# Attention in a four-layer kernel: score banks regrouped into two rings of three, exponentials taken in halves

## The chip, the cores and the metric

One core of one Trainium2 chip runs the whole program. The metric is the device time of one execution in microseconds. The kernel before took 611.96 us in the median of three runs (610.57 to 614.04).

## The reference, cut to what matters

Four layers follow each other on x of shape 16 x 128 x 256; each adds its result, scaled by tanh of a gate, to x: a WKV recurrence, a ternary feed-forward layer, a cross attention, a mixture of eight experts. The change is in the third:

```python
# target: layernorm(x), source: ctx; per batch 128 channels x 256 positions; HEADS = 16, HEAD_DIM = 8
q = einsum('oc,bct->bot', Wq, target) + bq     # k and v the same way from source
dot = einsum('bhdt,bhds->bhts', q, k) / sqrt(HEAD_DIM)
mask = target_mask[:, :, :, None] * source_mask[:, :, None, :]
dot = mask * dot - (1.0 - mask) * NEG
amap = softmax(dot, axis=-1) * mask
out = einsum('bhts,bhds->bhdt', amap, v)
```

So a batch has 16 heads, each with a 256 x 256 matrix of scores.

## The kernel before, in words

**Phases.** Up to about 180 us the first two layers run. The attention runs from there to about 447 us, its first two batches' scores beside the end of the feed-forward layer (the prologue). The experts follow.

**Attention by batch.** Every score is computed twice. First as rows by target position, in order that VectorE may take the maximum over the sources (`dve_reduce`, L907, one instruction for a head: 128 x 512 columns in, two maxima out). The negated maxima of a batch go through TensorE (`pe_mxT`, L841), ScalarE (`act_nm`, L975), GpSimd (`pool_np`) and memory and come back as three more rows of the stacked operand `QKA`. Then the scores are computed again, turned (rows by source position, the maximum already subtracted, `score_T`, L787), ScalarE takes the exponential (`act_exp`, L982) into `PT`, and TensorE multiplies by the values (`pe_pv`, L853), whose sums and products land in one bank, `PVB`.

**Order.** It is written by hand, as a slot for each batch b and pair p = 0 to 7; every engine walks the same slots in order (`turns`). The groups of batches 0 to 3 and 12 to 15 are unrolled, those between are a loop. In slot p of batch b TensorE does `pe_both`: the scores of heads n = 2p and 2p+1 (in the order of `head_of`) of batch b+2, and, between them matmul by matmul, four turned scores of batch b. Then it does `pe_pv` of two slots before, and in some slots one more piece of work, which shares the bank `MISC`: in slot 0 the maxima's transpose and before slot 1's pair the last value group of batch b-1, in slot 1 the projections of batch b+4 (L759, L763, the latter waits for VectorE's normalised row `Z3`, L893), in slot 3 the transpose of the result of b-1 (`pe_yT`, L862, after ScalarE's `act_qk`, L958, has read `MISC`), in slot 5 its transpose back (`pe_yo`, L869), in slot 6 the value projection (`pe_v`, L767, after VectorE's addition to X, L943). VectorE does two maxima in each slot and in slot 0 the statistics, in slot 1 `Z3`, in slot 3 and 4 the division (L918, L920, L926, L934, L938), in slot 5 the addition, in slot 7 `VF` (L899). ScalarE does one exponential in each slot, and `act_nm` in slot 0, `act_av` (L987) ahead of slot 1's, `act_qk` after slot 2's, `act_part` (L969) after slot 3's and 5's. The first `act_part` waits for GpSimd's masking of QK (L994), which waits for `act_qk`.

**Banks.** PSUM has eight banks of 512 fp32 columns. Before the change the scores for the maxima have two (`SBK`, banks 0 and 1, head n in bank n % 2). The turned scores have two double banks (`TBK`, banks 2 to 5, one double bank for a slot's four matrices). Banks 6 and 7 are `PVB` and `MISC`. `score_bank` lets TensorE write the scores of head n only when the maximum of head n-2 is taken (semaphore `a_red`); `turned_bank` lets it write a slot's turned scores when the exponential of two slots before is done (`a_exp`). In the last two batches there are no scores for maxima (`pe_scoresT`), and the layer norm of the experts and its transposes (L177) are in the slots.

Of the kernel before, what the change touches and what calls it, by code (L numbers as in the profile page):

```python
# [9 lines left out]
ACT = mybir.ActivationFunctionType  # L10
AX = mybir.AxisListType

P = 128
B, C = 16, 256
NG, GB = 4, 4
# [3 lines left out]
HEADS, HD = 16, 8  # L19
T = 256  # L20
# [29 lines left out]
def flamingo_kernel(nc, x, ctx, mask, g_xattn, g_ffn, time_decay, time_first, gate_wT, up_wT, down_wT,  # L50
# [10 lines left out]
    with ExitStack() as keep:  # L61
# [123 lines left out]
        with ExitStack() as part:  # L185
# [493 lines left out]
            with ExitStack() as att:  # L679
# [72 lines left out]
                def later(count):  # L752

                    return not isinstance(count, int) or count > 0
# [21 lines left out]
                def head_of(n):  # L776

                    return n // 2 + HALF * (n % 2)

                def score(pe, k, n, tt, SBK):  # L780
                    rows, h = rows_of(head_of(n))
                    return pe.matmul(SBK[n % 2][:, tt * T:(tt + 1) * T], QKA[rows, k, 0, h, tt * P:(tt + 1) * P],  # L782
                                     QKA[rows, k, 1, h, :], start=True, stop=True)

                def score_T(pe, k, i, st, j):
                    rows, h = rows_of(4 * j + i)
                    return pe.matmul(TBK[st][:, j * T:(j + 1) * T], QKA[rows, k, 1, h, st * P:(st + 1) * P],  # L787
                                     QKA[rows, k, 0, h, :], start=True, stop=True)

                def score_bank(pe, g, k, n):  # L790

                    b = GB * g + k
                    if n == 0:
                        pe.wait_ge(a_qa[k], 32 * (g + 1))
                    if later(HEADS * b + n - 1):
                        pe.wait_ge(a_red, HEADS * b + n - 1)

                def turned_bank(pe, g, k, i, st):

                    n = 8 * (GB * g + k) + 2 * i + st  # L800
                    if i == 0 and st == 0:
# [4 lines left out]
                def pe_scores(pe, g, k, p, SBK=SBK):  # L806

                    score_bank(pe, g, k, 2 * p)
                    score_bank(pe, g, k, 2 * p + 1)
                    for tt in range(2):  # L810
                        for n in (2 * p, 2 * p + 1):
                            last = score(pe, k, n, tt, SBK)
                            if tt == 1:
                                last.then_inc(a_s, 1)

                def pe_scoresT(pe, g, k, i, st):

                    turned_bank(pe, g, k, i, st)
                    for j in (0, 2, 1, 3):
                        last = score_T(pe, k, i, st, j)  # L820
                    last.then_inc(a_st, 1)

                def pe_both(pe, to_score, to_turn, p):


                    i, st = p // 2, p % 2
                    score_bank(pe, *to_score, 2 * p)
                    score(pe, to_score[1], 2 * p, 0, SBK)
                    turned_bank(pe, *to_turn, i, st)
                    score_T(pe, to_turn[1], i, st, 2)  # L830
                    score(pe, to_score[1], 2 * p, 1, SBK).then_inc(a_s, 1)
                    score_T(pe, to_turn[1], i, st, 3)
                    score_bank(pe, *to_score, 2 * p + 1)
                    score(pe, to_score[1], 2 * p + 1, 0, SBK)
                    score_T(pe, to_turn[1], i, st, 0)
                    score(pe, to_score[1], 2 * p + 1, 1, SBK).then_inc(a_s, 1)
                    score_T(pe, to_turn[1], i, st, 1).then_inc(a_st, 1)

# [5 lines left out]
                def pe_pv(pe, g, k, i, st):  # L844
# [5 lines left out]
                    grp = 0 if i < 3 else 1  # L850
                    pe.wait_ge(a_exp, 8 * b + 2 * i + st + 1)
                    for j in range(4):
# [48 lines left out]

                def dve_reduce(dve, g, k, n, SBK=SBK):
# [4 lines left out]
                    dve.tensor_reduce(MX[:, par, head_of(n), :], SBK[n % 2][:, :].rearrange("p (a s) -> p a s", a=2),  # L907
                                      axis=AX.X, op=ALU.max).then_inc(a_red, 1)
# [68 lines left out]
                def act_exp(act, g, k, i, st):  # L977
                    n = 8 * (GB * g + k) + 2 * i + st
# [913 lines left out]
```

## Time and profile before

| | |
|---|---|
| median of three runs | 611.96 us |
| the profiled execution | 612.62 us, of which the traced span is 610.9 us |
| TensorE / VectorE / ScalarE / GpSimd busy in the span | 83% / 67% / 37% / 34% |
| maxima (L907), 256 of 128 x 512 | 166.7 us, 682 ns each |
| exponentials (L982), 128 of 128 x 1024 | 129.9 us, 1023 ns each |
| scores (L782) and turned scores (L787), 512 matmuls each | 86.3 us and 84.9 us of TensorE's busy time |
| TensorE's clock over the span | 0.97 of full |

How to read it: the span is the trace's own clock from the first to the last instruction. Busy shares are over the whole program, four layers with different limits; what the change is worth has to be read inside the attention. An instruction's length in the trace can overlap its neighbour's on the same engine, so what an engine can do in a row is read from starts, not from lengths.

### The profile page before, as it was taken

How to read it: one execution, taken by the hardware profiler on the slowest of the kernel's cores; microseconds unless marked ns; L12 is line 12 of the kernel's file. 1: busy time of each engine (PE TensorE's matmuls, PEld its weight loads, DVE VectorE, ACT ScalarE, POOL GpSimd, SP SyncE). 2: the span in 40 equal slices, each digit the busy share in tenths (PEclk: the TensorE clock that was granted, in tenths of full speed). 3: DMA queues.
4: the chain of work that ended last, by engine and by line, in shares of the span. 5: the costliest groups of instructions: out<-in, count | busy, mean ns of one | idle time of the engine just before them, and what ended most of it. 6: DMA issues, size and time to landing. Idle time of an engine off the chain costs nothing. (4 is left out here: it accounts for less than half of the span.)

```text
span 610.9 us, 10613 instructions
## 1 busy us (share of the span) xinstructions
PE 508.4 (83%) x3368; PEld 269.3 (44%) x3368; DVE 407.8 (67%) x881; ACT 228.1 (37%) x330; POOL 205.7 (34%) x350
## 2 busy tenths in 40 slices
PE   1159899999798879999999998989879999899960
PEld 1034554644453433333333433333333555788850
DVE  4978678687535778888888888886946333333224
ACT  1003012031032027777777777767611010132310
POOL 2514115132265134554545545531210710022220
PEclk9999999999999969999999999999979999999995
DMA  6602006673228334555555555530040220266518
GB/s 165 213 1 69 1 0 134 88 188 141 58 70 224 87 93 134 154 148 148 149 138 140 137 136 153 140 83 7 3 141 2 103 69 0 66 187 190 185 40 275
DMA packets 70882, 68.11 MB, mean 111 GB/s; under 512 B 9136, under 2 KB 63328, under 8 KB 70848
## 3 DMA queue, kind: packets, MB, share of 16 engines
q1 hardware_dynamic: 69312, 63.48, 38.9%
q0 software_dynamic: 1536, 4.20, 1.9%
q8 instruction: 18, 0.29, 0.2%
q14 instruction: 16, 0.13, 0.1%
HBM read 41.04 MB, written 26.62 MB: 111 GB/s over the span
## 5 line engine op out<-in xcount | busy, mean ns | idle before, releaser
L907 DVE TENSOR_REDUCE MX<-psum 128x2 f32<-128x512 f32 x256 | 166.7, 682 | 32.0 <-PE psum L782 32.0
L982 ACT ACTIVATE HP<-psum 128x1024 f32<-128x1024 f32 x128 | 129.9, 1023 | 56.5 <-PE psum L787 54.6
L782 PE MATMUL psum<-QKA 60*128 60x256 bf16 x512 | 86.3, 279 | 21.0 <-DVE MX L907 19.4
L395 PE MATMUL psum<-space_a,space_w 128*128 128x512 f32 (+1 forms) x192 | 89.8, 616 | 5.0 <-ACT space_a L384 2.9
L787 PE MATMUL psum<-QKA 60*128 60x256 bf16 x512 | 84.9, 276 | 0.2 <-ACT HP L982 0.2
L853 PE MATMUL psum<-HP,VP 128*32 128x256 f32 x1024 | 81.8, 393 | 0.3 <-issue 0.2
L782 PEld LDWEIGHTS psum<-QKA 60*128 60x128 bf16 x512 | 33.5, 95 | 82.0 <-DVE MX L907 68.1
L395 PEld LDWEIGHTS psum<-space_a,space_w 128*128 128x128 f32 (+1 forms) x192 | 34.4, 187 | 49.1 <-issue 39.1
L431 PE MATMUL psum<-space_w,HP 128*128 128x256 f32 x192 | 50.8, 402 | 2.2 <-DVE HP L417 2.2
L1629 PE MATMUL psum<-space_a,wsh 128*128 (+3 forms) x96 | 45.2, 622 | 1.1 <-PEq L1120 1.1
L1703 PE MATMUL psum<-XT,WE 128*128 128x256 f32 (+1 forms) x192 | 44.1, 380 | 1.6 <-ACT XT L1584 1.6
L1557 POOL DMA_INDIRECT combined<-OE,to_u x16 | 15.3, 959 | 87.4 <-ACT OE L1597 85.0
L431 PEld LDWEIGHTS psum<-space_w,HP 128*128 128x128 f32 x192 | 33.9, 193 | 16.5 <-issue 12.4
L1703 PEld LDWEIGHTS psum<-XT,WE 128*128 128x128 f32 (+1 forms) x192 | 34.2, 181 | 8.2 <-issue 1.1
L403 ACT ACTIVATE space_a<-psum,hgs 128x512 f32<-128x512 f32 (+1 forms) x24 | 16.5, 686 | 56.5 <-PE psum L395 56.5
L1012 POOL TENSOR_TENSOR VP<-VF,maskT 128x32 f32<-128x32 f32 x128 | 25.9, 239 | 28.0 <-DVE VF L899 14.8
L145 POOL TENSOR_TENSOR rstd<-veps,neghalf 128x1 f32<-128x1 f32 (+1 forms) x21 | 15.7, 748 | 54.5 <-DVE veps L127 44.4
L787 PEld LDWEIGHTS psum<-QKA 60*128 60x128 bf16 x512 | 31.1, 95 | 6.1 <-issue 2.9
L994 POOL TENSOR_TENSOR QK<-QK,MB 128x512 f32<-128x512 f32 x16 | 20.3, 1268 | 40.0 <-ACT QK L958 40.0
L409 DVE SCALAR_TENSOR_TENSOR space_a<-space_a,psum 128x512 f32<-128x512 f32 (+1 forms) x24 | 16.1, 672 | 24.1 <-ACT space_a L403 24.1
L853 PEld LDWEIGHTS psum<-HP,VP 128*32 128x32 f32 x1024 | 20.4, 108 | 26.5 <-issue 22.0
L1837 DVE SCALAR_TENSOR_TENSOR H1s<-THs,psum 128x256 f32<-128x256 f32 (+1 forms) x24 | 10.1, 420 | 28.8 <-ACT THs L1591 27.8
(167 smaller groups left out, 710.3 us busy)
## 6 DMA issues: line engine op xcount, KB each, us to landing
QKA<-stack_scr SPq DMA_DIRECT2D x32, 480.0 KB, 5.3
stack_scr<-PARTS SPq DMA_DIRECT2D x32, 192.0 KB, 2.1
WE<-in_W SPq DMA_DIRECT2D x16, 352.0 KB
stack_scr<-PARTS SPq DMA_DIRECT2D x32, 128.0 KB, 1.9
dispatched<-zeros SPq DMA_DIRECT2D x8, 257.0 KB, 3.6
XD<-dispatched SPq DMA_DIRECT2D x8, 257.0 KB, 3.0
X<-in_x SPq DMA_DIRECT2D x4, 512.0 KB, 3.6
CV<-in_ctx SPq DMA_DIRECT2D x4, 512.0 KB, 4.6
```

The source lines that it names most:

```text
L395: last = pe.matmul(bank[2 * (i % 2) + side][0:m, :], (gw, uw)[side][:, h, i * P:i * P + m], ZT[:, h, :], start=(h == 0), stop=(h == 1))
L403: act.activation(TH[0:m, i % 2, :], bank[2 * (i % 2)][0:m, :], ACT.Tanh, scale=hgs[0:m, i:i + 1]).then_inc(s_th, 1)
L431: last = pe.matmul(DB[t // 2][:, (t % 2) * C:(t % 2 + 1) * C], HP[0:m, i, t * P:(t + 1) * P], dw[0:m, i, :], start=(i == 0), stop=(i == NI ...
L782: return pe.matmul(SBK[n % 2][:, tt * T:(tt + 1) * T], QKA[rows, k, 0, h, tt * P:(tt + 1) * P], QKA[rows, k, 1, h, :], start=True, stop=True)
L787: return pe.matmul(TBK[st][:, j * T:(j + 1) * T], QKA[rows, k, 1, h, st * P:(st + 1) * P], QKA[rows, k, 0, h, :], start=True, stop=True)
L853: last = pe.matmul(PVB[32 * j:32 * j + 32, grp * T:(grp + 1) * T], VP[:, k, st, 4 * j + i, :], PT[:, i % 2, st, j, :], start=(i in (0, 3) ...
L907: dve.tensor_reduce(MX[:, par, head_of(n), :], SBK[n % 2][:, :].rearrange("p (a s) -> p a s", a=2), axis=AX.X, op=ALU.max).then_inc(a_red, 1)
L982: act.activation(PT[:, i % 2, st, :, :].rearrange("p j t -> p (j t)"), TBK[st], ACT.Exp)\
L994: pool.tensor_tensor(QK2, QK2, MB[:, k, :].unsqueeze(1).broadcast_to([P, 2, T]), ALU.mult).then_inc(a_masked, 1)
L1012: last = pool.tensor_tensor(dst, src, maskT[:, st, bass.ds(b, 1)].unsqueeze(2) .broadcast_to([P, 4, 8]), ALU.mult)
L1629: last = pe.matmul(bank[2 * i + side][0:m, :], (wsh1, wsh3)[side][:, h, i * P:i * P + m], ZT4[:, h, bass.ds(GT * g, GT)], start=(h == 0), ...
L1703: last = pe.matmul(bank[i][0:m, lo:lo + CAP], w[:, s, h, i * P:i * P + m], XT[:, s, h, :], start=(h == 0), stop=(h == 1))
```

## The change: what it does

The scores for the maxima get three single banks (0, 1, 2), and the turned scores get three single banks (3, 4, 5), each bank holding two matrices. Both use the same order of banks in a batch, `THIRDS`: 0, 1, 2 over and over for the first fifteen, and bank 1 for the sixteenth. `last_use(n)` is the last earlier use of the same bank, counted over batches. It is three back nearly everywhere, two back for n = 15 and for n = 1 (which comes after the sixteenth of the batch before), and four back for n = 0 and n = 2. A slot's four turned matrices now lie in two banks, `half` = 1 first and `half` = 0 second, numbered by `turned_at`: 2p and 2p+1 in slot p. Each half has its own semaphore count in both directions: TensorE signals `a_st` after each half, ScalarE takes one exponential over 512 columns for each half (256 of them where there were 128), and TensorE waits for the half's bank alone. The order of the matmuls in `pe_both` is as before. In `pe_scoresT` both banks are waited for ahead of the four matmuls. The prologue keeps its two banks (`PRO`).

```diff
-                TBK = [psum[:, 2 * 512:4 * 512], psum[:, 4 * 512:6 * 512]]
+                THIRDS = [n % 3 for n in range(HEADS - 1)] + [1]
+                SBK3, TBK3 = bank[0:3], bank[3:6]
+                def last_use(n):
+                    return max(m for m in range(-HEADS, n) if THIRDS[m % HEADS] == THIRDS[n])
...
+                def turned_at(i, st, half):
+                    return 2 * (2 * i + st) + 1 - half
...
                 def score_bank(pe, g, k, n):
...
-                    if later(HEADS * b + n - 1):
-                        pe.wait_ge(a_red, HEADS * b + n - 1)
+                    score_filled(pe, g, k, n)
+                    pe.wait_ge(a_red, HEADS * (GB * g + k) + last_use(n) + 1)
...
-                def turned_bank(pe, g, k, i, st):
+                def turned_bank(pe, g, k, i, st, half):
...
-                    if later(n - 1):
-                        pe.wait_ge(a_exp, n - 1)
+                    if later(HEADS * b + last_use(m) + 1):
+                        pe.wait_ge(a_exp, HEADS * b + last_use(m) + 1)
...
                 def pe_scoresT(pe, g, k, i, st):
-                    turned_bank(pe, g, k, i, st)
-                    for j in (0, 2, 1, 3):
-                        last = score_T(pe, k, i, st, j)
-                    last.then_inc(a_st, 1)
+                    turned_bank(pe, g, k, i, st, 1)
+                    turned_bank(pe, g, k, i, st, 0)
+                    score_T(pe, k, i, st, 2)
+                    score_T(pe, k, i, st, 0)
+                    score_T(pe, k, i, st, 3).then_inc(a_st, 1)
+                    score_T(pe, k, i, st, 1).then_inc(a_st, 1)
...
                 def pe_both(pe, to_score, to_turn, p):
...
+                    for n, half in ((2 * p, 1), (2 * p + 1, 0)):
+                        to = SBK3[THIRDS[n]]
+                        score_bank(pe, *to_score, n)
+                        score(pe, to_score[1], n, 0, to)
+                        turned_bank(pe, *to_turn, i, st, half)
+                        score_T(pe, to_turn[1], i, st, 2 * half)
+                        score(pe, to_score[1], n, 1, to).then_inc(a_s, 1)
+                        score_T(pe, to_turn[1], i, st, 2 * half + 1).then_inc(a_st, 1)
...
                 def act_exp(act, g, k, i, st):
...
-                    act.wait_ge(a_st, n + 1)
-                    if later(n - 3):
-                        act.wait_ge(a_pv, n - 3)
-                    act.activation(PT[:, i % 2, st, :, :].rearrange("p j t -> p (j t)"), TBK[st], ACT.Exp)\
-                        .then_inc(a_exp, 1)
+                    for half in (1, 0):
+                        m = turned_at(i, st, half)
+                        act.wait_ge(a_st, HEADS * b + m + 1)
+                        if half == 1 and later(n - 3):
+                            act.wait_ge(a_pv, n - 3)
+                        act.activation(PT[:, i % 2, st, 2 * half:2 * half + 2, :].rearrange("p j t -> p (j t)"),
+                                       TBK3[THIRDS[m]], ACT.Exp).then_inc(a_exp, 1)
```

## Rows read from the trace of the kernel before

**Rows 1.** Windows: us, busy (x) of PE PEld DVE ACT POOL; PEclk, DMA, GB/s

```profile
225.32:239.38 14.06, 13.24 (x133) 5.27 (x133) 11.13 (x21) 9.79 (x15) 7.44 (x16) 0.83 0.53 139
...
325.78:340.16 14.38, 13.15 (x151) 5.47 (x143) 12.41 (x31) 10.59 (x15) 7.44 (x16) 1.00 0.58 146
...
397.63:410.93 13.30, 11.79 (x147) 4.66 (x139) 11.48 (x25) 8.89 (x12) 3.34 (x12) 1.00 0.37 85
410.93:423.01 12.08, 10.79 (x139) 3.84 (x131) 9.86 (x22) 8.76 (x12) 1.72 (x4) 1.00 0.02 5
423.01:447.00 23.99, 19.86 (x235) 8.66 (x228) 16.10 (x61) 16.50 (x20) 5.23 (x7) 1.00 0.02 4
```

**Rows 2.** PE's weight loads in one batch: start, length, what, [idle before and its releaser]

```profile
327.65 0.30 PEld L763 LDWEIGHTS psum<-Z,wq 128*128 128x128 f32 x2 [0.81 <-DVE Z L893]
328.27 0.09 PEld L782 LDWEIGHTS psum<-QKA 60*128 60x128 bf16 x1 [0.33 <-DVE MX L907]
...
328.82 0.16 PEld L853 LDWEIGHTS psum<-HP,VP 128*32 128x32 f32 x8 [0.21 <-issue]
...
330.05 0.09 PEld L782 LDWEIGHTS psum<-QKA 60*128 60x128 bf16 x1 [0.41 <-DVE MX L907]
...
330.37 0.16 PEld L853 LDWEIGHTS psum<-HP,VP 128*32 128x32 f32 x8 [0.21 <-issue]
330.94 0.42 PEld L862 LDWEIGHTS psum<-ident,AV 128*128 128x128 f32 x4 [0.41 <-ACT QK L958]
331.53 0.09 PEld L782 LDWEIGHTS psum<-QKA 60*128 60x128 bf16 x1 [0.17 <-issue]
...
334.30 0.20 PEld L869 LDWEIGHTS psum<-ident,YA 128*128 128x128 f32 x2 [0.41 <-issue]
334.67 0.09 PEld L782 LDWEIGHTS psum<-QKA 60*128 60x128 bf16 x1 [0.17 <-issue]
...
335.95 0.52 PEld L767 LDWEIGHTS psum<-wv,CX 128*128 128x128 f32 x4 [0.41 <-issue]
336.60 0.09 PEld L782 LDWEIGHTS psum<-QKA 60*128 60x128 bf16 x1
...
338.70 0.09 PEld L782 LDWEIGHTS psum<-QKA 60*128 60x128 bf16 x1 [0.73 <-DVE MX L907]
...
340.38 0.09 PEld L782 LDWEIGHTS psum<-QKA 60*128 60x128 bf16 x1 [0.41 <-DVE MX L907]
```

**Rows 3.** VectorE in the same batch, in order of time

```profile
327.03 0.56 DVE L893 TENSOR_SCALAR Z<-X,mv,rstd 128x256 f32 x1
...
328.70 2.48 DVE L907 TENSOR_REDUCE MX<-psum 128x2 f32<-128x512 f32 x4 [0.51 <-PE psum L782]
331.64 0.21 DVE L918 RECIPROCAL RD<-psum 128x8 f32<-128x8 f32 x1 [0.45 <-PE psum L862]
...
337.02 0.69 DVE L907 TENSOR_REDUCE MX<-psum 128x2 f32<-128x512 f32 x1 [0.49 <-PE psum L782]
...
337.96 0.68 DVE L907 TENSOR_REDUCE MX<-psum 128x2 f32<-128x512 f32 x1
```

**Rows 4.** ScalarE in the same batch, in order of time

```profile
329.04 1.02 ACT L982 ACTIVATE HP<-psum 128x1024 f32<-128x1024 f32 x1 [1.26 <-PE psum L787]
329.96 0.83 ACT L958 ACTIVATE QK<-psum,bqk 128x256 f32<-128x256 f32 x2
...
332.25 0.63 ACT L969 ACTIVATE PARTS<-QK 128x512 bf16<-128x512 f32 x1 [0.55 <-POOL QK L994]
332.79 2.10 ACT L982 ACTIVATE HP<-psum 128x1024 f32<-128x1024 f32 x2
```

**Rows 5.** ScalarE before the attention: two neighbouring operations over 512 columns

```profile
163.65 1.08 ACT L384 ACTIVATE space_a<-psum 128x512 f32<-128x512 f32 x2 [15.75 <-PE psum L378]
```

**Rows 6.** Groups by line and shape: busy us, mean ns of one

```profile
L384 ACT ACTIVATE space_a<-psum 128x512 f32<-128x512 f32 x8 | 4.5, 595 | 66.3 <-PE psum L378 66.3
```

**Rows 7.** ScalarE in the tail: three neighbouring exponentials over 1024 columns

```profile
430.40 2.85 ACT L982 ACTIVATE HP<-psum 128x1024 f32<-128x1024 f32 x3 [1.54 <-PE psum L787]
```

More of the change, by code:

```diff
@@ L778, in head_of, with score @@
                     return n // 2 + HALF * (n % 2)
-                def score(pe, k, n, tt, SBK):
+                def score(pe, k, n, tt, to):
                     rows, h = rows_of(head_of(n))
-                    return pe.matmul(SBK[n % 2][:, tt * T:(tt + 1) * T], QKA[rows, k, 0, h, tt * P:(tt + 1) * P],
+                    return pe.matmul(to[:, tt * T:(tt + 1) * T], QKA[rows, k, 0, h, tt * P:(tt + 1) * P],
                                      QKA[rows, k, 1, h, :], start=True, stop=True)
@@ L786, in score_T, with score_filled, score_bank, pe_scores @@
                     rows, h = rows_of(4 * j + i)
-                    return pe.matmul(TBK[st][:, j * T:(j + 1) * T], QKA[rows, k, 1, h, st * P:(st + 1) * P],
+                    to = TBK3[THIRDS[turned_at(i, st, j // 2)]]
+                    return pe.matmul(to[:, (j % 2) * T:(j % 2 + 1) * T], QKA[rows, k, 1, h, st * P:(st + 1) * P],
                                      QKA[rows, k, 0, h, :], start=True, stop=True)
-                def score_bank(pe, g, k, n):
-                    b = GB * g + k
+                def turned_at(i, st, half):
+                    return 2 * (2 * i + st) + 1 - half
+                def score_filled(pe, g, k, n):
                     if n == 0:
                         pe.wait_ge(a_qa[k], 32 * (g + 1))
-                    if later(HEADS * b + n - 1):
-                        pe.wait_ge(a_red, HEADS * b + n - 1)
-                def turned_bank(pe, g, k, i, st):
-                    n = 8 * (GB * g + k) + 2 * i + st
-                    if i == 0 and st == 0:
-                        pe.wait_ge(a_mx[k], 32 * (g + 1))
-                    if later(n - 1):
-                        pe.wait_ge(a_exp, n - 1)
-                def pe_scores(pe, g, k, p, SBK=SBK):
-                    score_bank(pe, g, k, 2 * p)
-                    score_bank(pe, g, k, 2 * p + 1)
+                def score_bank(pe, g, k, n):
+                    score_filled(pe, g, k, n)
+                    pe.wait_ge(a_red, HEADS * (GB * g + k) + last_use(n) + 1)
+                def turned_bank(pe, g, k, i, st, half):
+                    b, m = GB * g + k, turned_at(i, st, half)
+                    if m == 0:
+                        pe.wait_ge(a_mx[k], 32 * (g + 1))
+                    if later(HEADS * b + last_use(m) + 1):
+                        pe.wait_ge(a_exp, HEADS * b + last_use(m) + 1)
+                def pe_scores(pe, g, k, p, SBK):
+                    for n in (2 * p, 2 * p + 1):
+                        score_filled(pe, g, k, n)
+                        if later(HEADS * (GB * g + k) + n - 1):
+                            pe.wait_ge(a_red, HEADS * (GB * g + k) + n - 1)
                     for tt in range(2):
                         for n in (2 * p, 2 * p + 1):
-                            last = score(pe, k, n, tt, SBK)
+                            last = score(pe, k, n, tt, SBK[n % 2])
                             if tt == 1:
@@ L906, in dve_reduce @@
                     dve.wait_ge(a_s, HEADS * b + n + 1)
[L907 removed]
+                    src = SBK[n % 2] if SBK else SBK3[THIRDS[n]]
+                    dve.tensor_reduce(MX[:, par, head_of(n), :], src[:, :].rearrange("p (a s) -> p a s", a=2),
                                       axis=AX.X, op=ALU.max).then_inc(a_red, 1)
```

18 lines of the change are left out of this document (4 added, 14 removed).

## The prediction, before the changed kernel was run

> **What bounds the kernel now.** I read the busy times by stretch first. One batch of the steady attention takes 14.38 us, and no engine fills it: TensorE is shown 13.15 busy, VectorE 12.41, ScalarE 10.59 [rows 1]. So I went through one batch on each engine in order of time; the reader should compare each start with the end of what released it. VectorE stands idle for some 2 us, in four places [rows 3]: before the maximum of head 4 (0.51), before the reciprocals (0.45), before head 14 (0.49), and once more before head 2, half a microsecond after the pair that starts at 340.38 [rows 2]. TensorE in turn waits for VectorE before most pairs (0.41 to 0.73) and for Z3 before the projection (0.81) [rows 2]. The batch is a loop through both engines, ScalarE beside it with 3.8 us to spare.
>
> **What the steps last.** I count from the start of a pair's scores, and from starts, not lengths. On TensorE [rows 2]: an unhindered pair with its turned scores 0.55 (328.27 to 328.82), its second half until the value group 0.32, so the first half 0.23; a value group 0.57; the result's transpose 0.59; the transpose back 0.37; the value projection 0.65; the q projection 0.62; from head 1 over two value groups and the maxima's transpose to head 2, 1.68 (338.70 to 340.38). On VectorE [rows 3]: maxima follow each other by (2.48 - 0.68) / 3 = 0.60, and one starts 0.43 after its pair.
>
> **Three banks for the maxima: what goes.** Heads 6, 7, 10, 13 no longer wait for the maximum two before. Let t = 0 be the start of head 4 (328.27). Heads 6 and 7 end at 0.55 + 0.57 + 0.55 = 1.67, the value group at 2.24, so TensorE could transpose the result at 2.24 where it did at 2.67. But that also waits for `act_qk`, whose end is the next wait. Head 1 keeps its wait: it shares bank 1 with head 15 of the batch before, two back as before, and so does the projection's wait for Z3, and head 4 is behind that. These two stay whole: 337.96 to 338.70 is 0.74, and from head 2 over its maximum (0.43), Z3 (0.60 later), the q projection (0.62, 327.03 to 327.65) to head 4 (0.62) is 2.27.
>
> **Exponentials in halves: what is added.** 128 more instructions on ScalarE. Neighbouring operations over 512 columns took 1.08 for two [rows 5], each 0.595 long [rows 6], so 0.49 apart; exponentials over 1024, (2.85 - 1.02) / 2 = 0.92 apart [rows 7]. A slot costs 2 x 0.49 - 0.92 = 0.06 more, 0.5 us in a batch on an engine with 3.8 to spare: nothing in itself. What an exponential over 512 fp32 columns of PSUM costs when both its waits fall late the trace does not show; its ends are 0.49 (no cost beside the neighbour's) and 0.70 (the 0.60 of its length and a tenth for a wait that is not hidden). I take 0.49, by rows 5, which is the same shape and source. The first half can start 0.23 earlier than the whole did: 0.54 after head 4, not 0.77 (329.04 - 328.27) [rows 4].
>
> The Trainium skill, Perfetto Trace Analysis, section Optimizing Scalar/DVE Operations, gives some 51 ns of busy time for each further ScalarE instruction on PSUM, and advises grouping on a saturated engine; as an estimate from that page this would be 128 x 0.051 = 6.5 us of ScalarE time. The rows say 0.06 per added instruction, so page and trace agree; laid wholly on the path it would turn this change into a loss, but the same section allows breaking up where the engine isn't saturated.
>
> **Three banks for the turned scores: the wait that is added.** Before, a slot's turned scores waited for an exponential two slots back; there were four banks for them. Now the second half of slot p waits for the first half of slot p-1. Most slots don't feel it. Slot 5 does, since ScalarE is late there: exponentials at 0.54 and 1.03, `act_qk` at 1.52 (before: 1.69), ended at 1.52 + 0.83 = 2.35. The transpose of the result starts at about 2.45, not 2.24; so of the 0.43 gained, 0.2 stays, and VectorE still waits some 0.35 for it. `act_part` stood 1.46 behind the end of `act_qk` (329.96 + 0.83 to 332.25), for GpSimd's masking, so it starts at 3.81, the exponential of slot 4's first half 0.54 later (332.25 to 332.79) at 4.35 [rows 4], and ends at 4.95. TensorE wants to write the second half of slot 5 at 2.45 + 0.59 + 0.55 + 0.57 + 0.23 = 4.39 and may at 5.02. Queued behind it on TensorE are head 11's second matmul, the value group and the transpose back, and VectorE's addition behind that.
>
> **The new period.** From 5.02: value group 5.34, transpose back 5.91, head 12 6.28, value projection 6.28 + 0.55 + 0.57 = 7.40, head 14 8.05, its maximum 8.48, head 15's maximum 0.94 later (337.02 to 337.96) 9.42, head 1 at 10.16, head 2 at 11.84, head 4 at 14.11. The period is 14.1 instead of 14.38: 0.28 less. It applies to eleven batches (1 to 11): 3.1 us. VectorE would still be idle some 1.7 us per batch.
>
> **The other stretches.** Batch 0 has part of its time at TensorE's lower level, 1.2 GHz (PEclk 0.83 over the batch [rows 1]), where TensorE leads and a third bank helps less: 0.2. Batch 12 (13.30) has no projection, no `act_qk` and no `act_part`, so the new wait doesn't arise. From head 2: maxima at 0.43, 1.03, 1.63 (head 4), head 7 at 2.37, head 7's maximum at 3.43, the reciprocals right behind at 4.03, head 8's maximum 4.35, the transpose back at about 6.26, VectorE's addition done 7.73, value projection 7.79, head 14 8.44, its maximum 8.87, head 15's 9.81, head 1 at 10.55, head 2 at 12.23. That is 1.0 less. Batch 13 (12.08, VectorE busy 9.86) I put at half of that, 0.5. In the tail a slot becomes a ring through both engines: turned scores, 0.45, first half 0.60 long, 0.06 back: 1.11 against the 0.92 of [rows 7]. This holds for some three slots, until the result of batch 13 is transposed in slot 3 and VectorE has work; then VectorE's layer norm leads again (16.10 of 23.99 busy [rows 1]). Loss 0.5. The prologue and the other layers are not touched.
>
> Sum against the profiled execution: 612.62 - 3.1 - 0.2 - 1.0 - 0.5 + 0.5 = 608.3. That execution was 0.66 above the median of the runs, so I forecast 607.7.
>
> **The rivals.** (A) The turned wait doesn't bite, because ScalarE and GpSimd come earlier than the chain above. For it: TensorE missed the bank by 0.63 only, and a tenth less on each of several steps dissolves it. Then the value projection waits for VectorE's addition, some 0.42 earlier than above; the period is 13.7, eleven times 0.7 = 7.7, in all 612.0 - 7.7 - 0.3 - 1.5 + 0.5 = 603. Against it: GpSimd's 1.46 is seen in this batch and can't shrink by the change.
> (B) The new wait eats all that the third bank gives. With exponentials 0.60 apart (no overlap), `act_qk` ends at 2.57, `act_part` starts at 4.03, the exponential ends at 5.22 and slot 5's second half starts at 5.29, 0.27 later than above: period 14.38. What is left are batches 12 and 13 less the tail: 611. For it: no row shows exponentials of this size with two waits each.
> (C) Slower: the ring of turned banks becomes the bound. It decides as soon as slot 5's second half starts later than 5.02 + 0.28 = 5.30. With 0.70 apart `act_qk` ends at 2.77, `act_part` starts at 4.23, the exponential ends at 4.97 + 0.60 = 5.57, the period is 14.73; eleven times +0.35 = 3.9, nothing gained in batches 12 and 13, and the tail with some eight slots led by ScalarE loses 8 x 0.3 = 2.4: 618. Against it: ScalarE has 3.8 us idle in each batch, though not in the right place.
> Of the ring that frees banks one by one, the Trainium skill (Perfetto Trace Analysis, section Optimizing Tensor Performance) says that independent matmul groups should rotate through banks so that reading one overlaps writing the next; that would speak for A in both rings. The idle time before the maxima agrees for the first ring; for the second, no turned score waits in this batch (TensorE's waits in [rows 2] name VectorE), so there the change can only add.
>
> **How the numbers follow.** Forecast 0.40 (its own range 605.5 to 610), A 0.17, B 0.24, C 0.16, something else 0.03. The measurement can tell about 0.5%, 3.1 us, from no change: faster means below 608.9. All of A and three quarters of the forecast's share lie there: 0.47. Same (608.9 to 615.0) takes the rest of the forecast, B and the near side of C: 0.38. Slower 0.15. The range 602.5 to 614.5 takes in A and B and ends within C.
>
> **What would show it.** Right: batches some 14.1 us apart by the maxima's negation on ScalarE, a wait of turned scores (the line that was L787) on ScalarE's exponential once a batch in slot 5, about 0.6 long; head 1's wait on head 15's maximum unchanged; Z3 still waited for; exponentials about 0.49 apart where ScalarE runs on; batch 12 about a microsecond shorter. Wrong: exponentials 0.6 or more apart; turned scores waiting in several slots; VectorE's idle time below 1 us per batch, or a stretch of lower clock that was not there before.

## The result, and the profile after

The changed kernel takes 609.28 us in the median of 20 runs (607.09 to 614.05), the kernel before 612.14 (610.48 to 615.77). The ratio is 0.9956, 95% interval 0.9938 to 0.9974: faster by 0.44%, beyond its uncertainty, and just short of the 0.5% that the prediction called telling. The forecast was 607.7. The profiled execution took 611.10 us with a span of 609.4. The rows of the page that answer to the table of before (busy us, share, count; then line, engine, operation, busy us, mean ns, idle before):

```profile
PE 503.5 (83%) x3368; PEld 272.1 (45%) x3368; DVE 408.3 (67%) x881; ACT 235.7 (39%) x458; POOL 205.7 (34%) x350
...
L921 DVE TENSOR_REDUCE MX<-psum 128x2 f32<-128x512 f32 x256 | 166.5, 682 | 29.9 <-PE psum L787 29.8
L999 ACT ACTIVATE HP<-psum 128x512 f32<-128x512 f32 x256 | 138.7, 600 | 42.8 <-PE psum L793 42.0
```

The maxima cost what they did. The exponentials are 256 of 600 ns where there were 128 of 1023: 138.7 us instead of 129.9. VectorE's idle time before the maxima went from 32.0 us only to 29.9 on the page.

The busy time by stretch, one batch each, the last row the tail (stretch, length, busy of PE, PEld, DVE, ACT, POOL, then PEclk, DMA, GB/s), answers to [rows 1]:

```profile
226.41:240.25 13.84, 13.22 (x133) 5.37 (x131) 11.30 (x22) 10.60 (x23) 7.45 (x16) 0.81 0.55 139
240.25:254.15 13.90, 12.55 (x147) 5.47 (x150) 12.42 (x30) 10.98 (x22) 7.43 (x16) 1.00 0.58 159
...
296.41:311.06 14.65, 12.72 (x147) 5.71 (x150) 12.73 (x30) 10.76 (x23) 7.47 (x17) 1.00 0.53 129
...
339.15:353.33 14.18, 12.49 (x147) 5.45 (x143) 12.44 (x30) 10.99 (x23) 7.44 (x16) 1.00 0.55 145
...
395.52:408.46 12.94, 11.43 (x143) 4.90 (x146) 11.02 (x25) 9.25 (x18) 3.36 (x13) 1.00 0.40 91
408.46:420.43 11.97, 10.50 (x139) 4.18 (x138) 9.88 (x23) 9.27 (x20) 1.72 (x4) 1.00 0.03 6
420.43:446.00 25.57, 20.40 (x236) 8.84 (x228) 16.28 (x61) 18.07 (x35) 5.22 (x7) 1.00 0.01 4
```

Measured between the maxima's negations, eleven steady batches took 155.27 us where they took 158.25: 13.90, 13.90 and 13.98 in the unrolled group, 14.38 and 14.65 next, then 13.98 to 14.18 in the rest. Batch 0 gave 0.22, batch 12 0.36, batch 13 0.11. The tail, from the last negation to the last `act_av`, went from 22.93 to 24.25. (The last row of the table runs on to 446.00, hence its 25.57; the expectations below count the tail in that way.) In sum the attention, from the negation that opens batch 0 to the last `act_av`, takes 218.27 us instead of 220.62, 2.35 less. Before it 1.1 us is lost: that negation stands at 226.41 instead of 225.32. The change leaves the layers before alone; in this execution TensorE was granted 0.87 of its full clock between 165 and 185 us, in the one before 0.91.

One steady batch on TensorE's weight loads, [rows 2] after; head 4 starts at 341.82 (the first line, 304.15, is another batch's, whose head 4 starts at 299.16):

```profile
304.15 0.09 PEld L793 LDWEIGHTS psum<-QKA 60*128 60x128 bf16 x1 [0.66 <-ACT HP L999]
...
341.82 0.09 PEld L787 LDWEIGHTS psum<-QKA 60*128 60x128 bf16 x1 [0.33 <-DVE MX L921]
...
344.23 0.42 PEld L875 LDWEIGHTS psum<-ident,AV 128*128 128x128 f32 x4 [0.60 <-ACT QK L972]
...
346.99 0.09 PEld L793 LDWEIGHTS psum<-QKA 60*128 60x128 bf16 x1 [0.84 <-ACT HP L999]
...
347.88 0.20 PEld L882 LDWEIGHTS psum<-ident,YA 128*128 128x128 f32 x2 [0.41 <-issue]
...
349.36 0.52 PEld L772 LDWEIGHTS psum<-wv,CX 128*128 128x128 f32 x4 [0.41 <-DVE X L957]
...
352.11 0.09 PEld L787 LDWEIGHTS psum<-QKA 60*128 60x128 bf16 x1 [0.88 <-DVE MX L921]
...
353.79 0.09 PEld L787 LDWEIGHTS psum<-QKA 60*128 60x128 bf16 x1 [0.41 <-DVE MX L921]
```

The same batch on ScalarE, [rows 4] after:

```profile
342.36 1.09 ACT L999 ACTIVATE HP<-psum 128x512 f32<-128x512 f32 x2 [1.12 <-PE psum L793]
343.33 0.84 ACT L972 ACTIVATE QK<-psum,bqk 128x256 f32<-128x256 f32 x2
...
345.83 0.63 ACT L983 ACTIVATE PARTS<-QK 128x512 bf16<-128x512 f32 x1 [0.67 <-POOL QK L1011]
346.36 2.04 ACT L999 ACTIVATE HP<-psum 128x512 f32<-128x512 f32 x4
```

and on VectorE, [rows 3] after:

```profile
344.93 0.21 DVE L932 RECIPROCAL RD<-psum 128x8 f32<-128x8 f32 x1 [0.19 <-PE psum L875]
...
348.47 0.42 DVE L957 TENSOR_TENSOR X<-X,psum 128x256 f32 x1 [0.17 <-PE psum L882]
...
350.44 0.69 DVE L921 TENSOR_REDUCE MX<-psum 128x2 f32<-128x512 f32 x1 [0.35 <-PE psum L787]
```

The new wait stands at 346.99: the second half of slot 5's turned scores, 0.84 idle behind a ScalarE exponential, 5.17 behind head 4. The chain of the prediction can be read off: exponentials at 0.54, `act_qk` at 1.51, `act_part` at 4.01, exponentials of slot 4 at 4.54. This batch is not the common case, though. In six of the eleven steady batches `act_part` starts at 3.81 to 3.83 and the wait ends at 4.98 or 4.99 (304.15 - 299.16 = 4.99); in the three of the unrolled group it ends at 4.82. In the batch shown and in the loop's first, where it ends at 5.38, GpSimd began its masking of QK 0.19 and 0.40 later behind `act_qk` than in the six; why, the trace does not show. Head 1, at 352.11, still waits for head 15's maximum, 0.88. Before the reciprocals VectorE is idle for 0.19 instead of 0.45, before head 14 for 0.35 instead of 0.49.

What the prediction did not have are the maxima's return and the exact tail. In batches 5 and 12 turned scores waited more than a microsecond for the transfer of the maxima into QKA (a third such wait, 0.66 in batch 6, left the batch at 13.98). Those two, then the waits in batch 13 and in the tail, all TensorE weight loads:

```profile
309.58 0.09 PEld L793 LDWEIGHTS psum<-QKA 60*128 60x128 bf16 x1 [1.21 <-DMA QKA<-max_scr]
...
407.03 0.09 PEld L793 LDWEIGHTS psum<-QKA 60*128 60x128 bf16 x1 [1.15 <-DMA QKA<-max_scr]
...
417.84 0.09 PEld L787 LDWEIGHTS psum<-QKA 60*128 60x128 bf16 x1 [1.12 <-DVE MX L921]
...
422.06 0.14 PEld L793 LDWEIGHTS psum<-QKA 60*128 60x128 bf16 x4 [1.22 <-ACT HP L999]
...
423.21 0.14 PEld L793 LDWEIGHTS psum<-QKA 60*128 60x128 bf16 x4 [0.64 <-ACT HP L999]
```

### The profile page after: what moved, and what is told of

Read it like the earlier page. It is cut to its first block and busy times, and to the rows that moved or that the text cites. A ratio compares the mean times of both kernels' runs of the same rounds, so it can differ in the third digit from the quotient of the medians.

```text
span 609.4 us, 10827 instructions
## 1 busy us (share of the span) xinstructions
PE 503.5 (83%) x3368; PEld 272.1 (45%) x3368; DVE 408.3 (67%) x881; ACT 235.7 (39%) x458; POOL 205.7 (34%) x350
## 5 line engine op out<-in xcount | busy, mean ns | idle before, releaser
L921 DVE TENSOR_REDUCE MX<-psum 128x2 f32<-128x512 f32 x256 | 166.5, 682 | 29.9 <-PE psum L787 29.8
L999 ACT ACTIVATE HP<-psum 128x512 f32<-128x512 f32 x256 | 138.7, 600 | 42.8 <-PE psum L793 42.0
L395 PE MATMUL psum<-space_a,space_w 128*128 128x512 f32 (+1 forms) x192 | 91.1, 624 | 5.0 <-ACT space_a L384 2.8
L787 PE MATMUL psum<-QKA 60*128 60x256 bf16 x512 | 81.4, 278 | 15.5 <-DVE MX L921 13.9
L793 PE MATMUL psum<-QKA 60*128 60x256 bf16 x512 | 79.4, 276 | 10.5 <-ACT HP L999 7.8
L787 PEld LDWEIGHTS psum<-QKA 60*128 60x128 bf16 x512 | 35.2, 95 | 62.1 <-DVE MX L921 40.7
L793 PEld LDWEIGHTS psum<-QKA 60*128 60x128 bf16 x512 | 33.1, 95 | 21.0 <-ACT HP L999 13.5
L384 ACT ACTIVATE space_a<-psum 128x512 f32<-128x512 f32 x8 | 4.6, 596 | 67.0 <-PE psum L378 67.0
```

Of the source, the lines that this page charges most:

```text
L395: last = pe.matmul(bank[2 * (i % 2) + side][0:m, :], (gw, uw)[side][:, h, i * P:i * P + m], ZT[:, h, :], start=(h == 0), stop=(h == 1))
L787: return pe.matmul(to[:, tt * T:(tt + 1) * T], QKA[rows, k, 0, h, tt * P:(tt + 1) * P], QKA[rows, k, 1, h, :], start=True, stop=True)
L793: return pe.matmul(to[:, (j % 2) * T:(j % 2 + 1) * T], QKA[rows, k, 1, h, st * P:(st + 1) * P], QKA[rows, k, 0, h, :], start=True, stop=True)
L921: dve.tensor_reduce(MX[:, par, head_of(n), :], src[:, :].rearrange("p (a s) -> p a s", a=2), axis=AX.X, op=ALU.max).then_inc(a_red, 1)
L999: act.activation(PT[:, i % 2, st, 2 * half:2 * half + 2, :].rearrange("p j t -> p (j t)"), TBK3[THIRDS[m]], ACT.Exp).then_inc(a_exp, 1)
```

## The experiments

Ratios are to the kernel before, timed on the same chip, with 95% intervals. The changed kernel itself (0.9956) was not timed again on these chips, so a difference between two ratios carries both intervals. Batch times, tails and lengths of the attention (first negation of batch 0 to the last `act_av`, 218.27 us in the changed kernel) are of the profiled execution.

**What each part is worth.** First the turned ring and the halves without the third score bank:

```diff
-                    pe.wait_ge(a_red, HEADS * (GB * g + k) + last_use(n) + 1)
+                    pe.wait_ge(a_red, HEADS * (GB * g + k) + n - 1)
...
-                        to = SBK3[THIRDS[n]]
+                        to = SBK[n % 2]
```

> The changed kernel with its score ring put back to two banks (head n in bank n % 2, waiting for the maximum two before); the turned ring of three single banks and the exponentials in halves stay. My theory: the third score bank is what gains, and the turned ring gives nothing back by itself. Then a steady batch takes at least the 14.38 us of the kernel before, slot 5 waits little for the exponential (the score waits alone already bring it to about 5.1 us behind head 4), and the tail of the changed kernel (25.6 us instead of 24.0) stays: 613 to 614 us. Rival: the gain comes from the halves, since the first exponential starts 0.23 us earlier and act_qk behind it too; then a batch stays at 13.9 to 14.1 us and the time at 609 to 610.

Measured: 613.58 us, ratio 1.0033 (1.0015 to 1.0051); batches 14.38 to 14.54, tail 24.26. As expected. TensorE's waits for the maxima are back where they were; the first fence is the kernel before, the second this kernel, the third the changed one (engine, line, waited for, us in total, times, longest):

```profile
PEld psum L782 <- DVE MX L907: 56.0, 123, 0.8
```

```profile
PEld psum L787 <- DVE MX L921: 55.9, 122, 0.8
```

```profile
PEld psum L787 <- DVE MX L921: 29.7, 66, 1.1
...
PEld psum L793 <- DMA QKA<-max_scr: 3.0, 3, 1.2
```

So the third score bank gives 1.0033 to 0.9956, some 0.8%, and the turned ring with its halves takes 0.3%. Then the halves alone, with four single banks for the turned scores and the wait of four halves back:

```diff
-                    if later(HEADS * b + last_use(m) + 1):
-                        pe.wait_ge(a_exp, HEADS * b + last_use(m) + 1)
+                    if later(HEADS * b + m - 3):
+                        pe.wait_ge(a_exp, HEADS * b + m - 3)
...
-                                       TBK3[THIRDS[m]], ACT.Exp).then_inc(a_exp, 1)
+                                       bank[2 + m % 4], ACT.Exp).then_inc(a_exp, 1)
```

> The kernel before with nothing changed but the exponentials over 512 columns and a wait for each half: scores for the maxima in two banks, turned scores in a ring of four single banks. My theory: 128 further ScalarE instructions cost 0.06 us each on an engine with idle time, and the earlier start of the first half is worth little because the pairs still wait for the maxima: batch 14.3 to 14.4 us, total within 0.7 us of before (612.1), no extra time in the tail since four banks are there. Rival 1: the halves are what gains: 609 to 610. Rival 2: splitting costs about 0.2 us a slot on the path: 614 or more.

Measured: 612.24 us, ratio 1.0002 (0.9982 to 1.0021), batches 14.31 to 14.55, tail 23.12. 128 further instructions on ScalarE cost nothing beyond the interval, and starting the first half earlier gives nothing. In the trace the attention is 1.48 us longer than before (222.10 against 220.62), so a small cost is possible. The ring of three for the turned scores (223.15) adds another 1.05 to that, all of it in the tail, 24.26 against 23.12.

**The wait in slot 5.** `act_qk` ahead of slot 2's exponentials:

```diff
+                            if p == 2 and there(b, AHEAD_Q):
+                                act_qk(act, b + AHEAD_Q)
                             if there(b):
                                 act_exp(act, g, k, p // 2, p % 2)
...
-                            if p == 2 and there(b, AHEAD_Q):
-                                act_qk(act, b + AHEAD_Q)
```

> The changed kernel with one ScalarE step moved: act_qk of slot 2 stands ahead of that slot's exponentials instead of behind them. It attacks the chain that in the changed kernel holds slot 5's second half of turned scores (exponentials of slot 2, act_qk, GpSimd's masking, act_part, exponential of slot 4). My theory: act_qk starts about 0.15 instead of 1.5 us behind head 4, slot 5's wait for the exponential (0.6 to 0.8 us in each steady batch) disappears and the transpose of the result no longer waits for act_qk; a batch could take 13.7 us, total 605; but the maxima come back through memory just in time already (three waits of about 1 us for that transfer in the changed kernel), so this can give a part of it back: 605 to 608. Rival: slot 5's wait is not what sets the batch (head 1's wait for head 15's maximum, and Z3, are); then the batches stay at 13.9 to 14.1 and the time at 609.

Measured: 607.25 us, ratio 0.9928 (0.9908 to 0.9949). The wait in slot 5 shrank to 0.15 to 0.24 and batch 12 takes 12.56, but the steady batches stay at 14.05 to 14.21, a time I had given to the rival. The total is within the range given, yet no gain over the changed kernel is shown: the two intervals overlap, and the attention takes 218.84 us in this trace. The reason for the batch wasn't the rival's. One VectorE instruction grew from 0.18 to 0.70 us in eleven batches, and `pe_yo` behind it waited 1.04. VectorE, then GpSimd, in one of them:

```profile
358.49 0.70 DVE L940 TENSOR_TENSOR RD<-RD,maskG 128x32 f32<-128x32 f32 x1
```

```profile
357.98 1.16 POOL L1016 TENSOR_TENSOR QK<-QK,PARTS 128x512 f32<-128x512 f32 x1 [1.20 <-ACT PARTS L983]
```

It ends 0.05 us after GpSimd's subtraction: 358.49 + 0.70 = 359.19, 357.98 + 1.16 = 359.14. So next the subtraction was moved away from it:

```diff
-                            if p in (3, 5) and there(b, AHEAD_Q):
-                                act_part(act, b + AHEAD_Q, p // 2 - 1)
+                            if p in (4, 5) and there(b, AHEAD_Q):
+                                act_part(act, b + AHEAD_Q, p - 4)
```

> act_qk first in slot 2, as in the run before last, and besides the first act_part moved from slot 3 behind slot 4's exponentials. In the run with act_qk first VectorE's multiplication of the reciprocals by the mask (128 x 32, all three operands in SBUF) took 0.70 instead of 0.18 us in eleven batches, ending each time with GpSimd's subtraction that ran beside it, and the batch stayed at 14.1. My theory: that collision gives back what act_qk first gains; with act_part later GpSimd's subtraction falls behind the multiplication, which is 0.18 again, the transpose back no longer waits 1.04 for its input, and a batch takes 13.6 to 13.8: 602 to 605. Rival: the multiplication's length is hidden by other waits and the batches stay at 14.1: 607.

Measured: 605.67 us, ratio 0.9888 (0.9859 to 0.9917); the multiplication takes 0.18 again (179 to 191 ns in all sixteen), and the batches 13.50 to 13.85. The total is 0.7 above the range given. The attention takes 211.96 us, 6.3 less than in the changed kernel, although its tail took 25.14. That tail has another cause: from 422.69 to 427.69 the granted clock was 0.66, so TensorE spent part of the stretch at its lower level, 1.2 GHz; in the same stretch of the changed kernel's tail (429.43 to 434.43) it was 1.00. The run with `act_qk` first alone shows the same, 0.66 and a tail of 25.23, and TensorE was shown 6.39 us busy of the 9 us ahead of it, as in the changed kernel; why the clock fell there stays open. Whether it is the number of tensors that matters:

```diff
-                    ch.do(dve.tensor_tensor(rd, rd, maskG[:, :, bass.ds(b, 1)].broadcast_to([P, 2, HEADS]), ALU.mult))
+                    for tt in range(2):
+                        rd = RD[:, tt, :, :].rearrange("p j i -> p (j i)")
+                        last = dve.tensor_scalar(rd, rd, maskG[:, tt, bass.ds(b, 1)], None, ALU.mult)
+                    ch.do(last)
```

> The changed kernel with act_qk first (607.3, batch 14.1), and the multiplication of the reciprocals by the mask done as two instructions with one tensor and one number per partition (128 x 16 each) instead of one instruction on two tensors in SBUF. It tells what held that instruction for 0.70 us while GpSimd subtracted. My theory: an instruction with a single tensor from SBUF isn't held by GpSimd's work on two tensors, so the two take some 0.15 to 0.2 us each, the batch falls to 13.6 to 13.9 and the total to 603 to 605. Rival: any VectorE access to SBUF there waits for GpSimd's end; then the first of the two takes 0.5 us or more and the total stays at 607.

Measured: 610.63 us, ratio 0.9970 (0.9946 to 0.9993), batches 14.16 to 14.31. My theory fell, the rival's mechanism holds: the first of the two takes 0.67 or more, up to GpSimd's end. The time is 3.6 us above the rival's 607; the eleven batches are 0.1 us longer each than with `act_qk` first alone, 1.1 us of it, and the rest is open, for the attention as a whole takes no longer (218.62 us against 218.84). VectorE, then GpSimd, in one batch:

```profile
329.69 0.81 DVE L941 TENSOR_SCALAR RD<-RD,maskG 128x16 f32<-128x16 f32 x2
```

```profile
329.17 1.16 POOL L1018 TENSOR_TENSOR QK<-QK,PARTS 128x512 f32<-128x512 f32 x1 [1.19 <-ACT PARTS L985]
```

And the two ScalarE moves on the kernel before, with its two score banks:

> The kernel before (two score banks, double banks for the turned scores, exponentials over 1024 columns) with the two ScalarE moves alone: act_qk ahead of slot 2's exponential, the first act_part behind slot 4's. It tells whether these moves, which took the changed kernel from 609.3 to 605.7, gain by themselves. My theory: with two score banks the batch hangs on the waits for the maxima two before, so little is gained: batch 14.1 to 14.38, total 609.5 to 612. Rival: the moves gain by themselves and the third bank has no part in it: 608 or less.

Measured: 611.99 us, ratio 0.9992 (0.9976 to 1.0008), batches 14.38 as ever. Both moves together are worth 0.7% with three score banks and nothing that can be measured with two.

**Head 1's wait for head 15.** The short distances of both rings at heads 4 and 6:

```diff
-                THIRDS = [n % 3 for n in range(HEADS - 1)] + [1]
+                THIRDS = [0, 1, 2, 0, 2, 1, 2, 0, 1, 2, 0, 1, 2, 0, 1, 2]
```

> The changed kernel with the two short distances of both rings moved away from head 15 and head 1 (order of banks 0, 1, 2, 0, 2, 1, 2, 0, 1, 2, ...: now heads 4 and 6 come two after the last use of their bank, head 1 three after). My theory of the steady batch: it runs through slot 5's wait for the exponential and then through head 1's wait for head 15's maximum (0.88 us idle before head 1). If both links are in series, taking the second away shortens the batch by some 0.4 us where the maxima are back from memory in time: 604 to 607. But the maxima's return has almost no slack, so it may take the place: 608 to 609. Rival: head 1's wait is a mere consequence and gives nothing: 609.3, with the batch at 14.0.

Measured: 601.57 us, ratio 0.9825 (0.9795 to 0.9855); batches 13.05 to 14.15, batch 13 11.29, tail 23.70. One line gives three times what the whole change had given, and the trace has it in the attention, 210.47 us, 7.8 less. It moves the short distances of both rings at once, and no run moves one alone. The wait in slot 5 stays as it was (4.98 behind head 4 in most batches), and the tail, where only the turned ring is in use, gets 0.55 shorter, so most of the gain is put down to the score ring, but not measured apart. Head 1 (within the pair at 330.40) starts at once, and what waits in its stead is the projection, for Z3:

```profile
330.40 0.09 PEld L787 LDWEIGHTS psum<-QKA 60*128 60x128 bf16 x1 [0.41 <-issue]
...
330.95 0.16 PEld L866 LDWEIGHTS psum<-HP,VP 128*32 128x32 f32 x8 [0.21 <-ACT HP L999]
...
332.30 0.09 PEld L787 LDWEIGHTS psum<-QKA 60*128 60x128 bf16 x1 [0.41 <-DVE MX L921]
...
334.23 0.30 PEld L768 LDWEIGHTS psum<-Z,wq 128*128 128x128 f32 x2 [1.09 <-DVE Z L906]
```

With the two ScalarE moves besides:

> The kernel with act_qk first and act_part later, and besides the short distances of both rings moved as in the first kernel of this call. My theory: VectorE then has waits left only before head 2, head 4 (for Z3's sake) and a little elsewhere; a batch takes 13.1 to 13.5 us and the total is 598 to 602, unless the maxima's return through memory (store behind a 480 KB fill, 5.8 us to land) becomes the ring: then 602 to 604, and turned scores of slot 0 are seen waiting for that transfer in many batches.

Measured: 600.90 us, ratio 0.9807 (0.9781 to 0.9834). Batches 12.82 to 14.59, and turned scores wait for the maxima's return five times, 1.1 at most. By its waits this is the second case of what was expected, by its total the first: the waits are there, but cost less than I had thought. Beyond the 601.57 of the turned rings alone the two moves show no gain that stands clear of the intervals.

**The tail.** Four banks (`bank[2 + m % 4]`) and the wait of four halves back for the turned scores of the last two batches:

> The changed kernel with the turned scores of the last two batches, in which there are no scores for maxima, in a ring of four banks (2 to 5) again. My theory: the tail, 25.6 us in the changed kernel against 24.0 before, loses its 1.3 us since a slot's turned scores wait for the exponentials of two slots back again: 608 us, tail as before. Rival: the tail's length comes from the halves themselves (0.06 to 0.1 us a slot and one wait more each), then it stays at 25.6 and the total at 609.3.

Measured: 606.14 us, ratio 0.9902 (0.9881 to 0.9924), tail 23.12 instead of 24.25. The mechanism is right; the total moved 3.1 us, more than the 1.1 that the tail shows. In the profiled execution the attention takes 216.57 us, 1.7 less, and begins 5.05 us earlier (221.36), in layers that are the same in both kernels: between 165 and 185 us TensorE was granted 1.00 of its clock, 0.87 in the changed kernel's execution. So one edit's time can carry a clock that it did not cause; how much of the 3.1 that is stays open.

**The maxima's return.** Store and return ahead of the fill on SyncE's queue:

```diff
+                                sp_max_store(sp, *at(g, k, 1))
+                                sp_max_fill(sp, *at(g, k, 1))
                             if there(b, 3):
                                 sp_fill(sp, *at(g, k, 3))
```

> The changed kernel with another order on SyncE's queue: the maxima's store and its return to QKA stand ahead of the 480 KB fill for three batches later, instead of behind it. The store took 5.8 us to land in the median and 1.4 at best. My theory: in the changed kernel batches 5, 12 and some other start their turned scores late because the maxima aren't back (1.2 and 1.15 us waits in the profile, 3.0 in sum); with the store landing in about 2 us these waits go, steady batches stay at 13.9 to 14.1 and all of them are alike, batch 12 falls from 12.9 towards 12.3: 606.5 to 608. Rival: the fill comes later and becomes the wait in its place (scores of batch b+3 wait for it): 609 or more.

Measured: 613.82 us, ratio 1.0036 (1.0015 to 1.0056). The rival: no turned score waits for the maxima any more, but the scores wait for the fill, up to 3.1 us at a time:

```profile
PE psum L787 <- DMA QKA<-stack_scr: 9.1, 9, 2.6
...
PEld psum L787 <- DMA QKA<-stack_scr: 6.6, 5, 3.1
```

Everything that gained, together (act_qk first, `act_part` later, rings turned at heads 4 and 6, four banks in the tail):

> Everything that gained, together: the changed kernel with act_qk first, the first act_part later, the short distances of both rings moved to heads 4 and 6, and four banks for the turned scores in the last two batches. My theory: the gains in different stretches add up, 600.9 for the first three and 1 to 2 us for the tail: 598.5 to 600. Rival: the tail's VectorE work leads there now, and nothing is added: 601.

Measured: 600.58 us, ratio 0.9801 (0.9770 to 0.9832): nothing beyond the 600.90 without the tail's banks, so the rival's time, but not by its reason. The tail did get shorter, 23.15 against 23.70, and batch 13 longer, 12.23 against 11.30. The edit lets TensorE write the first turned scores of batch 14, which lie in a bank of the scores for the maxima, only when all maxima are taken (`pe.wait_ge(a_red, HEADS * B)`), and there TensorE stands idle until 0.06 behind the last maximum (407.42 + 2.48 = 409.90). The trace names no releaser; the time and the edit do. TensorE's weight load, then VectorE:

```profile
409.96 0.14 PEld L798 LDWEIGHTS psum<-QKA 60*128 60x128 bf16 x4 [1.33 <-issue]
```

```profile
407.42 2.48 DVE L933 TENSOR_REDUCE MX<-psum 128x2 f32<-128x512 f32 x4
```

In the kernel without the tail's banks TensorE is idle for 0.41 before the same scores. The wait of 1.33 is in the fastest kernel below, too. Last, the store alone ahead of the fill:

```diff
+                            if there(b, 1):
+                                sp_max_store(sp, *at(g, k, 1))
                             if there(b, 3):
                                 sp_fill(sp, *at(g, k, 3))
-                            if there(b, 1):
-                                sp_max_store(sp, *at(g, k, 1))
```

> The kernel of the run before this one, with the store of the maxima ahead of the 480 KB fill on SyncE's queue, but their return to QKA still behind it. With both ahead the fill came 2.6 us later and the scores for the maxima waited for it. My theory: the batches that wait for the maxima's return (five with 0.5 to 1.1 us) are put right since the store lands in about 2 us and not in 6, at the price of a fill some 1.3 us later; the batches get even, 13.0 to 13.3, and the total 596 to 599. Rival: the fill has no 1.3 us to spare, its waits come in the place of the others, and the total is 600 or more.

Measured: 598.15 us, ratio 0.9777 (0.9754 to 0.9800), the fastest, 2.2% below the kernel before; but the batches are not even (12.97 to 13.82). SyncE's queue, first in the changed kernel, then here (start, length of the issue; the maxima's store is `max_scr<-NP`, their return `QKA<-max_scr`, the fill `QKA<-stack_scr`, two transfers of 480 KB each):

```profile
300.14 0.97 SPq L1083 DMA_DIRECT2D QKA<-stack_scr  x2
301.24 0.32 SPq L1092 DMA_DIRECT2D max_scr<-NP  x1
...
307.52 0.61 SPq L1099 DMA_DIRECT2D QKA<-max_scr  x2
```

```profile
294.75 0.35 SPq L1104 DMA_DIRECT2D max_scr<-NP  x1
295.55 0.93 SPq L1095 DMA_DIRECT2D QKA<-stack_scr  x2
...
297.85 0.60 SPq L1111 DMA_DIRECT2D QKA<-max_scr  x2
```

The return is issued 6.3 us behind the store in the one and 3.1 in the other. TensorE's waits without this edit (the kernel of the run before), then with it:

```profile
PEld psum L798 <- DMA QKA<-max_scr: 3.6, 4, 1.4
```

```profile
PEld psum L798 <- DMA QKA<-max_scr: 1.2, 4, 0.4
...
PEld psum L787 <- DMA QKA<-stack_scr: 1.0, 1, 1.0
```

## Why the prediction was right, point by point

**Bound of the kernel before: right.** Two score banks made TensorE and VectorE wait for each other. With two banks neither the halves nor the ScalarE moves gain anything; with three both the bank and the moves do.

**Cost of the halves: right.** Four exponentials in a row took 2.04 us, so (2.04 - 0.60) / 3 = 0.48 apart; I took 0.49. So a slot costs 2 x 0.48 - 0.92 = 0.04 more, and ScalarE's busy time grew by 8.8 us for 128 instructions, 0.07 each. The ratio of the halves alone is 1.0002. The Trainium skill's 51 ns for each further instruction (Perfetto Trace Analysis, Optimizing Scalar/DVE Operations) lies between the two.

**The added wait: right in place and, where nothing else disturbs, in time.** Predicted 5.02 behind head 4 with `act_part` at 3.81; measured 4.98 or 4.99 with 3.81 to 3.83 in six of eleven batches. Where the maxima's return does not hold them up, these take 14.06 or 14.07 from head 4 to head 4 (predicted 14.11). The idle time is 0.57 to 0.66 in nine, 0.84 in the batch shown, 1.05 in the loop's first. That the mean of all eleven is 14.12, and their gain 2.98 us (3.1), is partly luck: without the two longest, 14.38 (the 1.05) and 14.65 (the maxima's return), the mean is 14.03. The prediction had neither. Batch 0 gave 0.22 (0.2).

**What was mis-sized.** Batch 12: 0.36 instead of 1.0. The walk through it left out the maxima's return, 1.15 us of wait at 407.03. Three kernels show the trade: with 1.15 of this wait batch 12 takes 12.94, with 0.76 (`act_qk` first) 12.56, with 0.34 (the mask in two instructions) 12.32, and the walk gave 12.3. The same wait, 1.21 us, stands in batch 5 with 14.65; in the kernel with four banks in the tail, the same in this stretch, it is 0.62 and the batch 14.07. The prediction has no term for SyncE's queue. In the kernel before no turned score waited for it; in the changed one three did. Batch 13: 0.11 instead of 0.5, a guess by half; it holds a wait of 1.12 at 417.84 before head 15, for the maximum of head 13, two back in the ring, and with the short distances moved it takes 11.3. Tail: 1.32 instead of 0.5. The ring of 1.11 us a slot was right (422.06 to 423.21 is 1.15), but I let it lead for three slots alone. Together 1.9 us too optimistic, the 4.3 forecast for the attention being 2.35 in the profile. The time itself came out 1.6 above the forecast, about as near to rival B's 611.

**The rivals.** A (603, batch 13.7) is what the kernel with `act_qk` first and `act_part` later came near to (605.7, 13.6); in the changed kernel the wait does bite. B needed the slot's second half at 5.29 and a batch of 14.38; it is 4.99 or earlier in nine of eleven batches, the mean batch is 14.12, and the 611 was missed by 1.7. C is refuted: exponentials are 0.48 apart, not 0.70, and the turned ring costs 0.3%, not 1%. Two sums in B and C do not follow from their own steps. With `act_part` at 4.03 and 4.23, 0.54 and 0.60 more give an exponential that ends at 5.17 and 5.37, not 5.22 and 5.57, and periods of 14.33 and 14.53. So B would have left 0.6 us of gain in the steady batches, and C would have been nearer 616 than 618. What the Trainium skill says of rotating banks (Perfetto Trace Analysis, Optimizing Tensor Performance) holds for the scores, where there was idle time to overlap; for the turned scores four banks were enough rotation already (1.0002 with the halves alone).

**What I priced at nothing and should not have.** I named head 1's wait for head 15 as a link that stays whole, and didn't ask what it was worth. It was the dearest link of those tried: moving the short distances of both rings, which adds no instruction, gives 1.3% on top of the change, though how much of that is head 1's wait alone was not measured.

## What to carry to other kernels

In a ring of buffers whose count doesn't divide the number of uses, somewhere the distance is short; put it where the producer is late anyway (here behind the projection), not where the consumer has extra work between two uses. When a bank is added in one ring by taking it from another, walk the other ring's chain through every engine in program order, to the first step queued behind something slow. When a stage gets shorter, look at transfers that were never waited for: they may have been hidden by exactly what is removed. And before a small difference is put down to an edit, look at the granted clock and at the stretches that the edit leaves alone.

## What the runs showed of the hardware

A small VectorE instruction on SBUF operands was held until a GpSimd instruction on SBUF operands had ended: 0.70 us instead of 0.18 for a multiplication of two tensors of 128 x 32, ending 0.05 us after GpSimd, in eleven batches of eleven where they met. With one tensor and one number per partition the same happened (0.67 to 0.71 where 0.22 is its own time). The multiplications that read PSUM (`YA`) and the maxima beside the same GpSimd instruction kept their times (beside the subtraction that starts at 346.54 in the changed kernel 0.22 for the last of the `YA` and 1.28 for two maxima, as without it).

On this the Trainium skill (SBUF — State Buffer) says, in the section Who interferes with whom, that the two engines share a pair of SBUF ports under an exclusive lock held for a whole instruction, which GpSimd takes, and so does VectorE with two SBUF inputs or in a two-port mode. The multiplication of two tensors agrees with this, 0.70 for 0.18; for the one with a number per partition no run here shows which of the two cases it was.

A 24 KB store behind two fills of 480 KB each on the same queue landed after 5.8 us in the median of sixteen, and after 1.5 ahead of them; 1.4 was the least in both.
